# A graph layer on Trainium2: the short last chunk of edges summed in the prologue, and the last groups in another order

## What is computed

```python
agg = segment_sum(edge_attr, dst, 12500)      # 200000 edges x 128, dst is sorted
h = relu(layernorm(x))                        # 12500 nodes x 128
h = concatenate([h, agg], -1)
h = relu(h @ W1 + b1)
h = relu(h @ W2 + b2)
h = h @ W3 + b3
out = x + layernorm(h) * ln_w + ln_b
```

## Time and profile before

| | us |
|---|---|
| median of three runs | 320.87 (320.09 to 321.0) |
| the profiled execution's own time | 320.3 |
| its span, first to last instruction | 318.4 |
| PE busy | 273.7 (86%) |
| DVE busy | 246.2 (77%) |
| POOL busy | 179.5 (56%) |
| ACT busy | 149.8 (47%) |
| moved by DMA | 116.49 MB, mean 366 GB/s |

### The profile page before, as it was taken

How to read it: one execution, slowest core, us unless ns; L and a number is a source line. 1 busy time by engine, 2 the same in 40 slices (tenths; PEclk the granted TensorE clock), 3 DMA queues, 4 the chain that set the end, 5 groups by cost and what they waited for, 6 DMA issues and landing times.

```text
span 318.4 us, 12666 instructions
## 1 busy us (share of the span) xinstructions
PE 273.7 (86%) x3927; PEld 186.3 (58%) x3927; DVE 246.2 (77%) x944; ACT 149.8 (47%) x407; POOL 179.5 (56%) x208
## 2 busy tenths in 40 slices
PE   2959998998988787999888888898888888898991
PEld 0736666665655555666556565565556565566560
DVE  4946588988778787588787977777787977777984
ACT  1542555555444444455444555544445555545632
POOL 8636555666545565266565665555565665555531
PEclk9977999999999999899999999999999999999997
DMA  7999999999999999999999999999999999999994
GB/s 245 344 379 371 373 371 372 373 386 373 386 373 379 381 373 386 373 374 372 373 373 373 373 374 372 373 373 373 373 373 373 373 373 373 373 373 374 376 399 158
DMA packets 81534, 116.49 MB, mean 366 GB/s; under 512 B 5392, under 2 KB 81520, under 8 KB 81520
## 3 DMA queue, kind: packets, MB, share of 16 engines
q1 hardware_dynamic: 80506, 115.86, 103.3%
q10 hardware_dynamic: 1014, 0.46, 0.5%
HBM read 109.90 MB, written 6.40 MB: 365 GB/s over the span
## 4 chain that ended last, share of the span: by engine, by line
SPq 52%; PE 18%; DMA 13%; issue 10%; DVE 5%; ACT 0%; POOL 0%; POOLq 0%; DVEq 0%
SPq L293 43%; DMA ring<-in_edge_attr 12%; PE part_ps L422 7%; SPq L288 5%; PE place_ps L433 3%; PE hid_ps L450 2%; PE y_ps L473 2%; PE hid_ps L457 2%; PE hid_ps L467 1%; DMA dst_i<-in_dst 1%; SPq L316 1%; SPq L320 1%; DVE local L884 1%; DVE least L882 1%; DVE span L887 1%
## 5 line engine op out<-in xcount | busy, mean ns | idle before, releaser
L784 POOL TENSOR_SCALAR place<-iota,rows_at 128x128 f32<-128x128 f32 x131 | 105.3, 808 | 104.8 <-PE place_ps L433 96.0
L422 PE MATMUL part_ps<-ring,onehot 128*32 128x128 f32 x3120 | 114.3, 281 | 26.0 <-DMA ring<-in_edge_attr 25.0
L422 PEld LDWEIGHTS part_ps<-ring,onehot 128*32 128x32 f32 x3120 | 79.0, 111 | 71.8 <-issue 50.5
L938 DVE TENSOR_TENSOR agg<-place_ps,agg 128x128 f32 x131 | 38.0, 290 | 52.7 <-PE place_ps L433 50.9
L433 PE MATMUL place_ps<-place,part 128*128 128x128 f32 (+1 forms) x262 | 64.7, 330 | 2.6 <-POOL place L784 2.3
L792 POOL TENSOR_TENSOR xs<-xs,vecs 128x384 f32 (+2 forms) x33 | 54.9, 1664 | 19.3 <-ACT h L653 19.3
L862 DVE TENSOR_TENSOR onehot<-iota,local_t 128x768 f32<-128x768 f32 x66 | 63.5, 964 | 0.3 <-issue 0.3
L639 ACT ACTIVATE part<-part_ps 128x128 f32<-128x128 f32 x131 | 35.0, 268 | 48.4 <-PE part_ps L422 46.7
L433 PEld LDWEIGHTS place_ps<-place,part 128*128 128x128 f32 (+1 forms) x262 | 40.0, 191 | 29.3 <-issue 22.4
L653 ACT ACTIVATE h<-xs,x_shift,x_rstd 128x128 f32 (+2 forms) x98 | 41.3, 483 | 2.4 <-DVE x_shift L855 2.4
L669 ACT ACTIVATE hid<-hid_ps,b1s 128x384 f32<-128x384 f32 (+1 forms) x33 | 19.0, 577 | 46.2 <-PE hid_ps L457 46.2
(11 more groups left out here) (86 smaller groups left out, 202.7 us busy)
## 6 DMA issues: line engine op xcount, KB each, us to landing
ring<-in_edge_attr SPq DMA_DIRECT2D x260, 384.0 KB, 9.2
xs<-in_x SPq DMA_DIRECT2D x32, 192.0 KB, 9.0
out_x<-xs SPq DMA_DIRECT2D x15, 384.0 KB
dst_i<-in_dst SPq DMA_DIRECT2D x1, 768.0 KB
ring<-in_edge_attr SPq DMA_DIRECT2D x1, 192.0 KB, 9.4
out_x<-xs SPq DMA_DIRECT2D x1, 192.0 KB
out_x<-xs ACTq DMA_DIRECT2D x1, 192.0 KB
xs<-in_x SPq DMA_DIRECT2D x1, 96.0 KB
```

Source lines behind the costliest of these rows:

```text
L422: last = nc.tensor.matmul(part_ps[par_q % 2][s * WIN:(s + 1) * WIN, 0:D], onehot[:, oct_par, first + s, j, :], e[:, s, j * D:(j + 1) * D], ...
L784: nc.gpsimd.tensor_scalar(place[:, par_q % 2, :], iota[:, 0:P], rows_at[:, k:k + 1], None, ALU.is_equal).then_inc(place_ready, 1)
L938: nc.vector.tensor_tensor(v, place_ps[par_q % 2][:, 0:P], v, ALU.add).then_inc(added, 1)
```

## The change

The left-over chunk gets tiles of its own (`tail_e`, `tail_i`, `tail_local`, `tail_onehot`), is loaded near the front of SP's order, and is summed in the prologue: DVE makes a dense one-hot of 128 nodes for each of its edges (3 x 128 columns), PE multiplies it in three 128x128x128 float32 products into `place_ps[1]`, and DVE adds that to the last 128 nodes of `agg`. Everything that quad "130" did in the tail goes. `layer1_*` of LAST use the bank `ht_ps` in place of `hid1_ps`. In the hand-written tail the order of PE, ACT and DVE is another, and in step 29 (`more_x`) `add(124)` moves ahead of `stats_x(31)`.

```diff
+TAIL_BASE = NODES - P
...
+        def layer1_bank(g):
+            return ht_ps if isinstance(g, int) and g == LAST else hid1_ps
...
 SP, prologue
+                sp.dma_start(tail_i[:, :], dst[TAIL0:EDGES].rearrange("(p j) -> p j", j=PER)).then_inc(tail_dst_loaded, 16)
...
                 load_x(0, 0, 0)
                 load_x(1, 1, 0)
+                sp.dma_start(tail_e[:, :, :], edges[TAIL0:EDGES, :].rearrange("(p j) f -> p j f", j=PER)).then_inc(tail_loaded, 16)
                 for q in range(1, RING):
...
 SP, after the last quad
-                    sp.wait_ge(seg_done, QUADS - RING + 1)
-                    tail = QUADS % RING
-                    sp.dma_start(ring[:, tail, 0:PER * D],
-                                 edges[TAIL0:EDGES, :].rearrange("(p j) f -> p (j f)", j=PER)).then_inc(edges_loaded[tail], 16)
...
 PE, start of the fast way
                     pe.wait_ge(wts_loaded, WTS)
+                    pe.wait_ge(tail_loaded, 16)
+                    pe.wait_ge(tail_onehot_ready, 1)
+                    for j in range(PER):
+                        last = nc.tensor.matmul(place_ps[1][:, 0:P], tail_e[:, j, :], tail_onehot[:, j, :],
+                                                start=(j == 0), stop=(j == PER - 1))
+                    last.then_inc(tail_summed, 1)
                     for q in range(AHEAD):
+                        if q == 2:
+                            pe.wait_ge(tail_added, 1)
                         if q >= 2:
...
 PE, tail
+                    put(q - 1, q - 1)
                     layer1_x(g)
+                    layer1_sums(g, q - 1)
                     seg(q, q, loads_of(q), q // 2 + 1)
-                    put(q - 1, q - 1)
-                    layer1_sums(g, q - 1)
+                    transpose_h(g + 1)
                     put(q, q)
-                    transpose_h(g + 1)
                     seg(q + 1, q + 1, loads_of(q + 1))
                     layer2(g)
...
                     layer1_sums(g + 1, QUADS - 1)
                     put(q + 3, q + 3)
-                    slot = QUADS % RING
-                    pe.wait_ge(onehot_ready, QUADS // 2 + 1)
-                    pe.wait_ge(edges_loaded[slot], loads_of(QUADS) - LANDED + 16)
-                    for j in range(PER):
-                        last = nc.tensor.matmul(part_ps[QUADS % 2][0:WIN, 0:D], onehot[:, (QUADS // 2) % 2, 0, j, :],
-                                                ring[:, slot, j * D:(j + 1) * D], start=(j == 0), stop=(j == PER - 1))
-                    last.then_inc(seg_done, 1)
+                    layer1_x(LAST)
                     layer2(g + 1)
-                    layer1_x(LAST)
-                    put(QUADS, QUADS, rows=WIN)
+                    layer1_sums(LAST, QUADS)
+                    layer3(g + 1)
+                    layer2(LAST)
                     layer3_last_bias()
-                    layer3(g + 1)
-                    layer1_sums(LAST, QUADS + 1)
-                    layer2(LAST)
                     layer3_last()
...
 ACT, tail
+                    relu1(g)
+                    y_sqrt(g - 1)
                     copy_part(q, q)
-                    relu1(g)
                     copy_ht(g + 1)
                     copy_part(q + 1, q + 1)
                     relu2(g)
-                    y_sqrt(g - 1)
                     copy_part(q + 2, q + 2)
                     copy_part(q + 3, q + 3)
                     relu1(g + 1)
                     y_sqrt(g)
-                    copy_part(QUADS, QUADS, rows=WIN)
                     relu2(g + 1)
...
 POOL
-                    rows_of(QUADS, 1, True)
-                    placement(QUADS, QUADS, 0, STEPS + 2)
...
 DVE, prologue
                 dve.wait_ge(local_t_ready, ROWT)
+                dve.wait_ge(tail_dst_loaded, 16)
+                nc.vector.tensor_scalar(tail_local[:, :], tail_i[:, :], float(TAIL_BASE), None, ALU.subtract).then_inc(tail_rebased, 1)
...
-                (two memsets to -1 in local_t)
+                (the same two in tail_local, after tail_rebased)
+                dve.wait_ge(tail_masked, 1)
+                nc.vector.tensor_tensor(tail_onehot[:, :, :], iota[:, 0:P].unsqueeze(1).to_broadcast([P, PER, P]),
+                                        tail_local[:, :].unsqueeze(2).to_broadcast([P, PER, P]), ALU.is_equal
+                                        ).then_inc(tail_onehot_ready, 1)
...
 DVE, fast way
                     dve.wait_ge(agg_zeroed, 1)
+                    dve.wait_ge(tail_summed, 1)
+                    v = agg[:, TAIL_BASE:NODES]
+                    nc.vector.tensor_tensor(v, place_ps[1][:, 0:P], v, ALU.add).then_inc(tail_added, 1)
+                    dve.wait_ge(tail_added, 1)
...
                         if more_x:
+                            add(q + 3, 0, base[3])
                             stats_x(i + 2, x_loaded[par], 16 * pairs + 32)
                             mean_x(i + 2)
-                        add(q + 3, 0, base[3])
+                        else:
+                            add(q + 3, 0, base[3])
...
 DVE, tail
                     take_y(g - 1)
                     add(q - 1, q - 1, base[0])
                     stats_y(g - 1)
                     mean_y(g - 1)
+                    center_y(g - 1)
+                    scale_y(g - 1)
                     add(q, q, base[1])
-                    center_y(g - 1)
-                    make_onehot(q // 2 + 2, 1)
+                    output(g - 1)
                     add(q + 1, q + 1, base[2])
-                    scale_y(g - 1)
-                    output(g - 1)
+                    take_y(g)
                     add(q + 2, q + 2, base[3])
-                    take_y(g)
                     stats_y(g)
                     mean_y(g)
+                    add(q + 3, q + 3, base[4])
                     center_y(g)
                     scale_y(g)
-                    add(q + 3, q + 3, base[4])
                     output(g)
-                    add(QUADS, QUADS, base[5])
                     take_y(g + 1)
```

More of the change, by code:

```diff
@@ L77, in gnn_kernel @@
 def gnn_kernel(nc, x, dst, edges, w1, b1, w2, b2, w3, b3, lnw, lnb, out):
-    assert GROUPS == 32 and QUADS == 4 * STEPS + AHEAD and LAST_P * LAST_PER == LAST_N and RC * RP == REST
+    assert CHUNKS * NODES_PER_CHUNK - SLACK >= TAIL_BASE and GROUPS == 32 and QUADS == 4 * STEPS + AHEAD and LAST_P * LAST_PER == LAST_N and RC * RP == REST
     with ExitStack() as ctx:
@@ L95, in gnn_kernel @@
         place = sb("place", [P, 2, P])
+        tail_e = sb("tail_e", [P, PER, D])
+        tail_i = sb("tail_i", [P, PER], I32)
+        tail_local = sb("tail_local", [P, PER])
+        tail_onehot = sb("tail_onehot", [P, PER, P])
         iota = sb("iota", [P, BANK])
@@ L170, in gnn_kernel @@
         local_t_ready = sem("local_t_ready")
+        tail_dst_loaded = sem("tail_dst_loaded")
+        tail_loaded = sem("tail_loaded")
+        tail_rebased = sem("tail_rebased")
         tail_masked = sem("tail_masked")
+        tail_onehot_ready = sem("tail_onehot_ready")
+        tail_summed = sem("tail_summed")
+        tail_added = sem("tail_added")
         base_ready = sem("base_ready")
@@ L358, in general @@
                                  dst[EDGES - REST:EDGES].rearrange("(p c) -> p c", c=RC)).then_inc(dst2_loaded, 16)
+                    sp.wait_ge(tail_loaded, 16)
                     for k in range(RING):
@@ L449, in layer1_x @@
                     t = h_t if n == CHUNK else h_last_t
-                    nc.tensor.matmul(hid1_ps[:, 0:n], w1x[:, :], t[:, :], start=True, stop=False)
+                    nc.tensor.matmul(layer1_bank(g)[:, 0:n], w1x[:, :], t[:, :], start=True, stop=False)
                 def layer1_sums(g, sums=None):
@@ L456, in layer1_sums @@
                         pe.wait_ge(added, sums)
-                    nc.tensor.matmul(hid1_ps[:, 0:n], w1a[:, :], agg[:, bass.ds(g * CHUNK, n)],
+                    nc.tensor.matmul(layer1_bank(g)[:, 0:n], w1a[:, :], agg[:, bass.ds(g * CHUNK, n)],
                                      start=False, stop=True).then_inc(hid1_done, 1)
@@ L668, in relu1 @@
                     act.wait_ge(hid1_done, g + 1)
-                    nc.scalar.activation(hid1[:, 0:n], hid1_ps[:, 0:n], ACT.Relu, bias=b1s[:, 0:1]).then_inc(hid1_ready, 1)
+                    nc.scalar.activation(hid1[:, 0:n], layer1_bank(g)[:, 0:n], ACT.Relu, bias=b1s[:, 0:1]).then_inc(hid1_ready, 1)
                 def relu2(g):
@@ L917, in _ @@
                 dve.wait_ge(local_t_ready, ROWT)
+                dve.wait_ge(tail_dst_loaded, 16)
+                nc.vector.tensor_scalar(tail_local[:, :], tail_i[:, :], float(TAIL_BASE), None, ALU.subtract).then_inc(tail_rebased, 1)
                 whole = DONE // PER
-                nc.vector.memset(local_t[0:whole, DONE % PER:PER, CHUNKS:CHUNKS + 1], -1.0)
-                nc.vector.memset(local_t[0:whole + 1, 0:DONE % PER, CHUNKS:CHUNKS + 1], -1.0).then_inc(tail_masked, 1)
+                dve.wait_ge(tail_rebased, 1)
```

(8 more changed lines are left out.)

## The result

| | before | changed |
|---|---|---|
| median of six runs | 320.86 us (320.09 to 321.55) | 324.25 us (323.1 to 325.3) |
| the profiled execution's own time | 320.3 | 325.3 |
| its span | 318.4 | 323.2 |
| mean granted PE clock | 0.977 | 0.961 |

The ratio is 1.0105, 95% interval 1.0075 to 1.0134: slower by 1%. The forecast was slower, 323.0, range 321.7 to 324.2. The measured median lies 0.05 above the range, and the change of +3.4 us is larger than the +2.4 forecast. The way is right, and the sum is short by 1 us. The profiled execution of the changed kernel is the slowest of its six, and that of the kernel before lies 0.56 under its median, so what follows shows more of the loss (+5.0 us) than the medians do.

A forecast was written before the change was run, and what follows sets the result against it. The DMA stream bounds the kernel to about 290 us, then PE's order, with DVE nearly full. Prologue 0, stream +0.73, stall +2.42, tail's end -0.71 sum to +2.44: 323.0 us on the mean of four (320.57), range 321.7 to 324.2.

The forecast's parts named there:

- Prologue, 0: Start of the kernel: the chunk's added DVE, PE and SP work hides in idle time and under the DMA queue, cost 0.
- the 0.6 to 1.2 of the rival: Prologue: the wait for `tail_added` and a longer lower-clock spell empty SP's queue, +0.6 to 1.2, 324.0 us; chance 0.05.
- The stream, +0.73: DMA stream: `tail_e` (0.53) and `tail_i` (0.20), loaded near the front, make landings at the end later, +0.73.
- The stall: Tail's beginning: `y_sqrt(29)` waits for `mean_y(29)` ahead of `copy_part(126)` on ACT, delaying `put(126)` and `seg(127)` on PE, +2.42.
- the stall doesn't bind: Tail's beginning: `mean_y(29)` ends early enough that `copy_part(126)` stays where it was; -0.3, 320.3 us; chance 0.11.
- the one in which the stream's shift doesn't reach PE either: No stall, and gaps in the prologue's DMA take `tail_e`; -1.04, 319.5 us; chance 0.04.
- The bound of +0.74 for `output(28)` meeting POOL: Tail's beginning: earlier `put(125)` releases POOL's `placement(127)` into DVE's `output(28)`, +0.74 at most, taken as 0.
- The 0.4 us that I worked out for this place from the Trainium skill: `output(28)` on DVE would wait out one POOL placement under the port-lock rule, some 0.4 us, making the sum 323.4.
- `seg(127)` to `seg(129)`, 4.38 as before: PE's tail behind the stall: old order, PE full in it, so the stretch keeps its 4.38 us.
- The tail's end, -0.71: From `seg(129)` to `take_y(31)`: `layer2(31)` gains 0.25 and `layer3(31)` gains 0.46, -0.71.
- The wait for `add(128)`: DVE's tail: `add(128)` behind `take_y(30)` should end just ahead of `layer1_sums(31)`; otherwise it costs a few tenths.
- `take_y(31)` to the end: Last stretch of the tail: the chain is DVE's from `take_y(31)` on and stays unchanged.

The follow-up runs named there:

- e3: Changed kernel with ACT and DVE of the tail, step 29, and PE up to `transpose_h(31)` in the old order: 320.05 us, ratio 0.9989.
- e1: Changed kernel with `y_sqrt(29)` back behind `relu2(30)` on ACT, all else as it is: 320.87 us, ratio 1.0005.
- e4: Kernel before with only `y_sqrt(29)` moved ahead of `copy_part(126)` on ACT: 322.61 us, ratio 1.0073.
- e6: Kernel before with four more loads of 192 KB, which nobody reads, ahead of quad 1: 321.81 us, ratio 1.0051.
- e7: Kernel before with eight more loads of 128 packets of 12 bytes, which nobody reads, ahead of quad 1: 321.23 us, ratio 1.0029.
- e8: Changed kernel unaltered, timed again beside the kernel before: 324.52 us, ratio 1.0148.
- e2: Changed kernel with three 128x128x384 products that nobody reads on PE between `transpose_h(31)` and `put(126)`: 322.7 us, ratio 1.0063.
- e10: Against e3, only DVE's step 29 and tail in the changed kernel's order: 320.18 us, ratio 0.9997.

## Why the prediction was wrong, and what in it was right

The stall that was forecast is there, in its place and size. The sum was short because it priced everything behind the stall at the higher clock. Step by step, in the profiled execution, forecast against measured:

- **Prologue, 0: right, as far as the runs can tell.** `seg(2)` was 0.67 late, and from the third slice on none of the prologue's moved less than 371 GB/s. e3, with the whole prologue in it, is 0.4 faster than the kernel before. Its other terms, +0.50 for the stream and -0.79 for the end, leave no room for the 0.6 to 1.2 of the rival.
- **The stream, +0.73: right in kind, too large.** The multiples give 0.38 + 0.12 = 0.50. The single row, +0.68, is not to be trusted to that accuracy.
- **The stall: right.** Forecast `mean_y(29)` at 301.02 and `put(126)` at 301.6, with the stream's 0.73 on top 301.75 and 302.33; measured 301.69 and 302.23. The rival "the stall doesn't bind" is out by e1 and e4, the one in which the stream's shift doesn't reach PE either also by e6 and e7. The bound of +0.74 for `output(28)` meeting POOL was not needed. POOL's two placements did come earlier and reached 0.28 into it, and it took 0.88 as before, in the timeline of the changed kernel:

```profile
297.31 1.19 POOL L798 TENSOR_SCALAR place<-iota,rows_at 128x128 f32<-128x128 f32 x2 [0.28 <-POOL rows_at L789]
...
298.22 0.88 DVE L1016 SCALAR_TENSOR_TENSOR xs<-z,y_rstd,xs 128x128 f32<-128x128 f32 x3
```

  The 0.4 us that I worked out for this place from the Trainium skill (page "SBUF — State Buffer", section "Who interferes with whom") is not in these rows. And one of the readings behind it was wrong: POOL's row of 1.40 in the old trace ends at 303.09, only 0.16 into `output(29)`. What lay beside most of that 1.62 is POOL's next row:

```profile
303.06 1.09 POOL L792 TENSOR_TENSOR xs<-xs,vecs 128x384 f32 x1
```

- **`seg(127)` to `seg(129)`, 4.38 as before: wrong, and this is the step that failed.** The text reads "PE was full in it, so it makes nothing good", which took the durations of the old trace for the new one. They hold at the higher clock only. The 2.2 us of idle time that the prediction itself had forecast took the clock to the lower level, and the same instructions took 6.95 (5.67 in e8, 5.71 in e4, and 4.39 in e2, where PE was kept busy). The 0.38 for `put(126)` was priced at the higher clock too. The prologue's rows at the lower clock, cited for the same `seg` (1.51 against 0.86), held the price: put on `seg(127)` alone, it would have given 0.65 more.
- **The tail's end, -0.71: right.** Measured -0.80, and -0.79 in e3; of the difference 0.08 is in `layer1_sums(31)`, which follows `seg(129)` by 0.79 and not by 0.87. The wait for `add(128)`, feared behind `take_y(30)`, shows in e1 and e10, where PE is not late already.
- `take_y(31)` to the end, forecast unchanged, took 0.36 less. Of that, 0.28 lies behind the start of `output(LAST)` (4.36 us to the end before, 4.08 after). Why is open; no run tries it.

The sum without the clock, +2.44, is what e2 measured: 322.7 - 320.45 = +2.25. (The filling ended 0.3 us before `put(126)` could start, so it took nothing.) The clock is the rest, as an estimate from medians of different chips: 1.1 us in the first measurement (3.4 - 2.25), 2.0 in the second (4.24 - 2.25). Each of these is uncertain by about 1 us: e2's interval alone goes from +1.5 to +2.6, that of the first measurement from +2.4 to +4.3. Range and chances were drawn round +2.44, with no case for it in the tail. I had it only as a part of the prologue's rival, where it costs nothing.

## What to carry to other kernels

Before moving an instruction ahead of another on an in-order engine, look up when the thing it waits for is ready in the old trace, and who stands behind it: here a 0.3 us square root, ready 2.4 us too late, stopped PE in a stretch where PE sets the time. When a forecast holds an idle time of PE, price what follows at the lower clock as well as at the higher, since the stretch after it cost up to 2.6 us on top of 2.2 to 2.4 of waiting, and in some executions of e4 it seems nothing; if the wait can't be taken away, work that nobody reads can be cheaper than none. And let a small gain (the chunk in the prologue with PE's new end, -0.4 us) be timed by itself before an order change is laid on top of it.

## What the runs showed of the hardware that I had not expected

- An idle time of PE of 2.23 us took the granted clock from 1.00 to 0.50. In the first profile it fell 1.6 us into the idle time and stayed low from 301.6 to 308.4, with PE busy for the last 6 us of it; in e8 it fell only as PE began again (0.96 in the mean from 302.0 to 302.5, 0.50 from 302.5) and was back by 306. Idle times of 0.78, at 296.31 in the kernel before and at the same place in e3, left it at 1.00. How much was lost differed from execution to execution of the same kernel (5.67 and 6.95 us for one stretch; 322.4 to 324.7 for e4), so one profile can't give its size.
- A load of 128 packets of 12 bytes cost 0.12 us at the end (e7), one of 128 packets of 1.5 KB 0.38 (e6), which is a ratio of 3 for a ratio of 128 in bytes.
